# Fewer plain jobs in the dense stages, one square root behind the scatters, and row transfers that wait for the first gathers, in an attention and mixture-of-experts block

## What is computed

```
h = layernorm(x) * (1 + ca) + sa
x = x + ga * attention(h)          # 16 heads of 8 features, q = k = v = h, 2 x 16 x 1024 x 1024 scores
h = layernorm(x) * (1 + cb) + sb
shared = relu(h @ sW1 + sb1) @ sW2 + sb2
probs  = softmax(h @ router_W + router_b)      # 15 experts
cw     = the 3 largest of probs per token, 0 elsewhere
y      = sum over e of cw[e] * (relu(h @ eW1[e] + eb1[e]) @ eW2[e] + eb2[e])
x = x + gb * (shared + y)
```

## Time and profile before

| | |
|---|---|
| median of 3 runs | 377.3 us (375.74 to 377.87) |
| profiled execution | 377.16 us; span 375.6 us |
| PE, ACT, DVE, POOL busy | 86%, 76%, 44%, 22% of the span |
| attention ends | about 261 us |
| tail: 10 groups of tiles | about 267 to 310 us |
| tail: dense stages, gathers and sums | about 310 to 370 us |

### The profile page before, as it was taken

The page is one execution under the profiler, slowest core; times in us unless marked ns, Lnnn a source line. Parts: engine busy times, 40 slices in busy tenths (PEclk is TensorE's granted clock), DMA queues, the critical chain, the costliest instruction groups (busy, mean ns, idle before and its releaser), DMA issues.

```text
span 375.6 us, 6507 instructions
## 1 busy us (share of the span) xinstructions
PE 321.9 (86%) x2355; PEld 146.2 (39%) x2355; DVE 164.9 (44%) x508; ACT 286.2 (76%) x284; POOL 82.7 (22%) x105
## 2 busy tenths in 40 slices
PE   4879799998999999899998999997599299999822
PEld 2632222222333223233222223321478296767521
DVE  7993014235152372442622303500265079877942
ACT  3679889999999999999999999997165265443311
POOL 4891001601000000100000656700010000067730
PEclk9999989999999999999999999999699699999985
DMA  7788899151000799700000011124844897912211
GB/s 219 253 316 293 276 364 307 48 188 66 3 2 0 268 308 391 241 0 2 3 0 2 29 38 49 51 80 125 268 113 117 249 384 230 384 39 77 83 31 61
DMA packets 37908, 55.94 MB, mean 149 GB/s; under 512 B 3888, under 2 KB 20818, under 8 KB 37232
## 3 DMA queue, kind: packets, MB, share of 16 engines
q1 hardware_dynamic: 35900, 51.92, 41.3%
q0 software_dynamic: 1536, 3.16, 3.0%
q10 hardware_dynamic: 436, 0.39, 0.3%
HBM read 34.92 MB, written 22.51 MB: 153 GB/s over the span
## 4 chain that ended last, share of the span: by engine, by line
issue 28%; PE 18%; POOL 13%; SPq 11%; DMA 11%; DVE 9%; ACT 8%; ACTq 1%; POOLq 0%; DVEq 0%
PE acc L1653 8%; ACT prob L840 7%; POOL xs_d L767 6%; SPq L574 5%; PE slot L1558 4%; SPq L575 4%; POOL QQ L778 4%; DMA val<-cw_d 3%; DMA xs_d<-xtok,line 2%; POOL val L778 2%; DMA cw_d<-cwT 2%; DMA KK<-kw 1%; PE slot L1713 1%; POOL rstd L689 1%; DMA kw<-w1l 1%
## 5 line engine op out<-in xcount | busy, mean ns | idle before, releaser
L840 ACT ACTIVATE prob<-slot 128x1536 f32<-128x1536 f32 x171 | 233.5, 1489 | 8.8 <-PE slot L1558 8.3
L1653 PE MATMUL acc<-prob,val 128*18 128x512 f32 x1024 | 136.4, 605 | 2.7 <-DVE oT L1145 1.8
L1558 PE MATMUL slot<-QQ,KK 32*128 32x512 f32 (+1 forms) x768 | 92.9, 410 | 11.6 <-ACT prob L840 8.2
L1558 PEld LDWEIGHTS slot<-QQ,KK 32*128 32x128 f32 x768 | 43.9, 187 | 130.0 <-ACT prob L840 93.9
L689 POOL TENSOR_TENSOR rstd<-rstd,power 128x4 f32<-128x4 f32 (+1 forms) x6 | 7.4, 1241 | 198.9 <-DVE rstd L984 198.9
L869 ACT ACTIVATE ghi<-prob 128x512 fp32r<-128x512 f32 x26 | 16.4, 632 | 31.5 <-DVE prob L1383 31.5
L1653 PEld LDWEIGHTS acc<-prob,val 128*18 128x18 f32 x1024 | 17.4, 96 | 31.9 <-issue 28.9
L778 POOL DMA_INDIRECT QQ<-ys_d,line x16 | 16.0, 1001 | 58.8 <-DMA val<-cw_d 54.2
L767 POOL DMA_INDIRECT xs_d<-xtok,line x24 | 23.9, 996 | 7.3 <-issue 6.4
L1145 DVE COPY oT<-acc 128x512 f32<-128x512 f32 x8 | 5.5, 692 | 42.9 <-PE acc L1653 42.9
L896 ACT ACTIVATE prob<-slot,rows 128x128 f32<-128x128 f32 x38 | 10.9, 373 | 11.0 <-DMA ys_d<-prob 6.5
(11 more groups left out here) (282 smaller groups left out, 359.9 us busy)
## 6 DMA issues: line engine op xcount, KB each, us to landing
KK<-wcat SPq DMA_DIRECT2D x32, 128.0 KB, 2.0
KK<-kd SPq DMA_DIRECT2D x14, 256.0 KB, 5.6
QQ<-qd SPq DMA_DIRECT2D x14, 256.0 KB, 6.0
KK<-kw SPq DMA_DIRECT2D x14, 256.0 KB, 6.4
KK<-cw_d SPq DMA_DIRECT2D x3, 1024.0 KB, 7.5
xs_d<-ffT SPq DMA_DIRECT2D x1, 2580.0 KB, 14.6
rows<-xs_d SPq DMA_DIRECT2D x10, 258.0 KB, 4.1
ys_d<-prob SPq DMA_DIRECT2D x10, 256.0 KB, 5.3
```

What stands on the lines that cost most here:

```text
L840: nc.scalar.activation(ring[:, at:at + n * CH], slot[u % 2][:, 0:n * CH], ACT.Exp, scale=SCALE).then_inc(exp_done, 1)
L1558: return mm(dst, KK[n][r, s, c * M:(c + 1) * M], QQ[n][r, lo:hi], start=True, stop=True, tile_position=(32 * q, 0))
L1653: last = mm(acc[32 * q:32 * q + 2 * HV], val[:, b, n // 2, c, q, HV * odd:HV * odd + 2 * HV], prob[:, (G * cl + q) % RING], start=c == 0 a ...
```

## The change

Three places change. `PLAIN` shrinks from positions 0, 6 and 11 to position 0, so four of the 32 jobs become split jobs, and two loads of 64 KB into `w2p` at the program's start go. POOL serves two square roots of 512 tokens, not three, before the scatters, and two, not one, behind them. And in the tail POOL's gathers of stage 0 wait for chunks 0 to 3 alone, SP's chunk 4 waits for those gathers (`gath[0]`), and the gathers of stage 1 wait for chunks 4 to 7. DVE's sums of stage 0 move from jobs 24 and 25 to jobs 16 and 22, and the first two sums of stage 1 from job 30 to behind the last job.

```diff
-PLAIN = (0, 6, 11)
+PLAIN = (0,)
...
             routing(1)
+            sp.wait_ge(gath[0], 16 * QC * K)
             for k in range(CHUNKS, DENSE * CHUNKS):
                 row_chunk(k)
...
-            for _ in range(LAST):
+            for _ in range(SORTED):
                 root_guess(0, QC)
...
-            root_guess(0, QC)
+            for _ in range(SORTED, STAGES):
+                root_guess(0, QC)
             for k in range(YRING):
                 pool.wait_ge(y_wr[k], 16 * len(range(k, GROUPS, YRING)))
-            for k in range(DENSE * CHUNKS):
-                pool.wait_ge(rows_ld[k], 16 * len(row_buffers(k)))
             pool.wait_ge(pv_done, CLASSES)
             for s in range(SORTED):
+                for k in range(CHUNKS * s, CHUNKS * (s + 1)):
+                    pool.wait_ge(rows_ld[k], 16 * len(row_buffers(k)))
                 for k in range(K):
                     for i in range(QC * s, QC * (s + 1)):
                         p.indirect_dma_start(yacc[s][k][:, i % QC], None, ys_d, line_of(i, k)).then_inc(gath[s], 16)
...
-                if g == EXPERTS + 8:
+                if g == EXPERTS:
                     three_results(0)
-                if g == EXPERTS + 9:
+                if g == EXPERTS + 6:
                     stage_sum(0)
-                if g == EXPERTS + 14:
-                    three_results(1)
+            three_results(1)
             stage_sum(1)
```

## The result

| | before | changed |
|---|---|---|
| median | 376.86 us (375.74 to 377.87, 4 runs) | 355.11 us (354.47 to 359.01, 4 runs) |
| profiled execution | 377.16 us, span 375.6 us | 359.01 us, span 357.3 us |
| PE, ACT, DVE, POOL busy | 86%, 76%, 44%, 22% | 89%, 80%, 47%, 23% |

The ratio is 0.945 [0.939, 0.951]: 5.5% faster. Every ratio in this document compares executions in the chip's faster state alone, with a 95% interval in brackets. The prediction was 360.4 us with a range from 356.5.

A forecast was written before the change was run, and what follows sets the result against it. PE and ACT bound the attention; then two PE holes and late gathers. Groups end 14.4 us earlier, the series behind takes 63.4 us, not 65.8: span 358.8, plus 1.6 gives 360.4 us, range 356.5 to 368.5.

The forecast's parts named there:

- Scatters and SP: POOL's scatters run from 187.9 to 223.7 us, 21.0 us earlier, again taking 35.8 us; SP's weights follow from 226.0.
- Rival C: Scatters stretch beside DVE's work between 188 and 208 us; unit 146 and all behind it 6 us later, 366.4; chance 0.06.
- F: Whole kernel: the gain is cancelled by a wait not seen, 377 us; chance 0.03.
- The two holes and the clock: PE's waits before the first tile and at group 0's store go: 4.9 and 7.1 us; faster clock 1.2 and 2.0.
- Rival B: The second hole, at group 0's store, stays in part; in full 369.5 us; chance 0.12.
- The new wait: At unit 146 PE waits 1.1 us for stage 2's normalised rows; 1.0 us charged at the attention's end.
- Gathers of stage 0: In the tail, twelve gathers until DVE sees the last take 16.6 us, as stage 1's did before.
- Stores and chunks in: Behind job 2, stores and chunks 0 to 3 land after 6.6 us in place of 7.3, bounds 5 to 8.5.
- The series: Tail's gathers, chunks 4 to 7, gathers set the end at 349.3; dense stages' last gate comes 4 us earlier, at 344.9.
- Split for plain: Down products in the jobs: 1.22 us plain against 1.18 split on PE; DVE's added low parts covered; no effect.
- The end: From DVE's last instruction to the end of the span, 5.8 us as before.
- Rival D: Chunks and gathers 1 us less in each link, nothing lost at unit 146: 354 to 357 us; chance 0.06.

The follow-up runs named there:

- the repetition: The whole change run again unaltered on another chip, against the kernel before: 356.51 us, ratio 0.945 [0.942, 0.949].
- the root between: Changed kernel with stage 2's square root between the second and third round of scatters: 356.06 us, ratio to the kernel before 0.943 [0.940, 0.947].
- the roots alone: Kernel before with only stage 2's square root moved behind the scatters: 359.9 us, ratio 0.955 [0.951, 0.959].
- the turns alone: Kernel before with only SP's wait, POOL's split wait and the new places of DVE's sums: 373.61 us, ratio 0.994 [0.991, 0.997].
- plain alone: Kernel before with only the list of plain products cut to position 0: 374.02 us, ratio 0.994 [0.991, 0.997].
- the late sums: Changed kernel without SP's wait before chunk 4 and with stage 0's sums at jobs 24 and 25: 348.86 us, ratio to the kernel before 0.927.

## Why the prediction was right and where it was wrong

The order of the waits and what ends each was right; several sizes were not. The columns are the predicted profile, the changed kernel's first profile, the one of the repetition and the last one.

| us | predicted | first | repetition | last |
|---|---|---|---|---|
| end of the attention | 262.3 | 260.3 | 259.0 | 259.4 |
| from there to job 2 | 33.1 | 32.2 | 32.2 | 32.2 |
| to stores and chunks in | 6.6 | 8.7 | 7.4 | 8.7 |
| to the first gather | 0.8 | 0.8 | 0.8 | 0.8 |
| gathers of stage 0, as DVE sees them | 16.6 | 17.8 | 18.0 | 18.0 |
| chunks 4 to 7, and to the next gather | 13.3 | 13.2 | 12.9 | 13.2 |
| gathers of stage 1 | 16.6 | 16.6 | 16.8 | 16.4 |
| last sums of DVE | 3.7 | 3.5 | 3.5 | 3.5 |
| from there to the span's end | 5.8 | 4.2 | 4.6 | 4.4 |
| span | 358.8 | 357.3 | 355.2 | 356.5 |

- **Scatters and SP.** Right. From the copies at 186.93 to the end of the last issue at 221.60 it took 34.7 us, where 35.8 were taken over from before; the weights followed 2.3 us later, as before. Rivals C and F are out. The 1.1 us that it was shorter are one pause between rounds of 1.38 us where the kernel before had 2.39, and no scatter of 1.48 us, less 0.4 for slower first copies.
- **The two holes and the clock.** Right: 32.2 us against 33.1 to job 2, with the clock at 1.00. Rival B is out. Group 0's store went out at 270.07 (predicted 272.1), when SP had just issued the last weights. The 0.8 us charged for stage 3's routing were not paid: from the first tile to job 2 the only wait in PE's timeline is 0.39 us.
- **The new wait, "I charge 1.0 us at the end of the attention".** Wrong in size. The rows were ready at 223.31 + 1.11 = 224.42 and PE took them at 224.57. They were 2.2 us earlier than the predicted 226.6, by the 1.1 us above and by a front 1.1 us ahead of the earlier trace rows. With no wait (the kernel before, and the one with the root between) PE's scores behind the side work start 1.08 us after those ahead of it; in the three profiles of the changed kernel it is 1.23, 1.39 and 1.24 us. So the wait was 0.15 to 0.31 us.
- **Gathers of stage 0, "I take what stage 1 took", 16.6.** 1.2 to 1.4 us too little. The first took 1.48 us in place of 0.94, and seven of the others came every 1.40 us, not every 1.26 (last section).
- **Stores and chunks in, "with the chunks spread more evenly I take 6.6".** 0.8 to 2.1 us too little. The last store took 8.20 us to land, where the one of before took 6.8. Spreading the chunks bought nothing. The loads of chunks 4 to 7 took 12.5, 12.1 and 12.4 us from first issue to last landing, as the trace of before had it (12.3). The 10.8 us estimated beside it were not reached; by the sizes in the profile the five loads have 3840 KB, which is 3.93 MB, and the estimate would be 11.0.
- **The series.** Right: it sets the end, stage 1's wait for a gather ends at 349.62 (predicted 349.3), and the dense wait came as 5.26 + 3.57 us on DVE, 5.48 us on PE. But its rival, the dense stages, was closer than the 4 us predicted: DVE waited only 1.64, 0.69 and 1.58 us for the last gather.
- **Split for plain, "nothing".** The reading of the costs was loose. 610 and 394 ns are lengths of records that overlap. By the starts, a job with a plain product took PE 1.56 us and a split one 1.40 (kernel before, 318.3 to 322.7 us), so a split product is the cheaper one by 0.16 us. It didn't reach the end, which the gathers set.
- **The end, "to the end of the span ... 5.8", taken over from before.** 1.2 to 1.6 us too much. The three undisturbed profiles of the kernel before have 5.8, 5.5 and 5.9 us there; the roots alone 5.8, the turns alone 4.4 and 4.5, plain alone 3.1 and 3.7. So this stretch was shorter with either smaller part, by 1.3 and by 2.0 to 2.6 us. If that is no chance of these few profiles, it is half of what the turns gained alone, and all of what the plain list did. But it does not add up: the changed kernel has both and is only 1.3 us shorter here. What happens there is only the last two stores of the output: the issue of one took 1.42 us before and 0.62 us after. Why was not settled.
- **The base.** The three undisturbed profiles of the kernel before end the attention at 261.3, 262.8 and 260.0 us, those of the changed kernel (the one with the root between counted) at 260.3, 259.0, 258.9 and 259.4. In the sum this is 2 us, and I had reckoned everything from the 261.3.

The windows of 40 to 50 us show where executions part (columns as in the earlier trace rows). The kernel before, the turns alone, the late sums:
```profile
40.00:50.00 10.00, 7.93 (x57) 2.04 (x57) 0.92 (x6) 7.51 (x6) 0.00 (x0) 0.83 0.91 307
```
```profile
40.00:50.00 10.00, 9.04 (x77) 2.63 (x81) 1.31 (x8) 10.00 (x9) 0.00 (x0) 1.00 0.93 301
```
```profile
40.00:50.00 10.00, 8.10 (x53) 2.15 (x49) 0.00 (x0) 6.54 (x5) 0.00 (x0) 0.69 0.90 303
```
ScalarE is busy for 7.51, 10.00 and 6.54 of 10 us, at a clock of 0.83, 1.00 and 0.69, in kernels whose programs differ nowhere up to 185 us but for two early loads. The attention then ended at 261.3, 258.7 and 262.7. So single executions differ by 4 us at the end of the attention, whatever the change, and in this window alone ScalarE's busy time differs by 3.5 us. The fastest version has as late a front as the kernel before had at its latest (262.8). That the changed kernel was early four times and the one before late three times is most likely chance: with the front of the kernel before, the turns alone ended the attention at 258.7 and the roots alone at 259.8, and with the front of the changed one the late sums ended it at 262.7. For the shorter list of plain products it took 109.5 us from the end of the attention to the last sum, with 108.6, 108.4 and 111.3 before. Its 0.6% isn't in the jobs, and no run here ties it to the stores by a mechanism.

**The sum.** By the means of these profiles, the span fell from 376.5 to 356.2, by 20.3 us: 2.0 in the front (predicted a loss of 1.0), 17.0 between the cuts (109.4 to 92.4; predicted 17.9), and 1.3 behind the last sum (predicted 0).

**The step that failed.** Three terms of the sum were too large: the charge of 1.0 us at unit 146 (measured 0.15 to 0.31), the 5.8 us at the end (4.2 to 4.6), and the base of 261.3 us, taken from one profile (258.9 to 260.3 in the changed kernel). Between the cuts the good agreement is partly luck: the groups took 0.9 us less than predicted, and stores and gathers of stage 0 2.2 to 3.5 us more. The range was added up from three terms only: it had no room for the base, for the end, or for the routing's own bounds of 0 to 2 us. (Its upper end by those three terms is 365.2, not 365.5.)

These terms explain the profiles, not the whole miss. The mean span of the four profiles is 356.2 us, 2.6 below the predicted 358.8. The measured median of 355.11 us stands for a span of about 353.4, another 2.8 us lower, and lies in executions without a profile. In which stretch they were quicker stays open. Rival D named the right time, 354 to 357, but for links of the series that did not get shorter; only its "nothing is lost at unit 146" came nearly true.

## What to carry to other kernels

When an answer that only one stage needs is computed ahead of a long run of transfers, see what is queued behind its request: moving one square root of 1 us behind 24 scatters gave 4.5%. The turns and the plain list gave 0.6% each when alone, which a repetition of an unchanged kernel hardly tells from nothing, and 0.9% together on top of the square root. On the chip where the attention was stretched beside the scatters, the square root's gain was gone, by one execution of each kernel. Turn-taking between gathers and loads moves the wait: the run without it showed that the loads could be hidden (4 us), and the run with later sums that DVE's own order held 3 us more. In that fastest version DVE is busy for 4.8 to 5.0 of every 5 us from 325 to 345 us, so whether it would gain from a longer plain list again, with fewer low parts for DVE, is open: it wasn't run. Anchor a prediction on more than one profile, and give the start and the end of the span a spread of their own.

## What the runs showed of the hardware

Of stage 0's gathers, seven in a row took 1.09 to 1.10 us and came every 1.40 us, where most of the kernel before took 0.95 to 0.96 and came every 1.26. Timeline of DVE in the changed kernel beside the gathers at 306.44 and 307.84:
```profile
306.04 0.68 DVE L1393 SCALAR_TENSOR_TENSOR glo<-prob,ghi 128x512 fp32r<-128x512 f32 x1
306.77 0.75 DVE L1385 SCALAR_TENSOR_TENSOR prob<-slot,bcol,KK 128x512 f32<-128x512 f32 x1
307.44 0.68 DVE L1393 SCALAR_TENSOR_TENSOR glo<-prob,ghi 128x512 fp32r<-128x512 f32 x1
```
DVE's loop has a period of 1.40 us too, so POOL had fallen into step with it. In the kernel with the root between, the first six gathers beside the same loop still came every 1.26 us, and only from the seventh on every 1.40. Once DVE stopped at 314.5, they took 0.95 us again. In stage 1, where DVE's loop had a period of 1.26 us, ten of twelve took 0.94 to 0.96. So the price seems to depend on how the two loops stand to each other, not on DVE being busy alone.

The Trainium skill (SBUF — State Buffer, section "SBUF: two separate sides") says that the two engines take turns on a shared port pair. The trace fits this: a gather that falls into step with DVE's loop takes 0.14 us more, and the twelve of stage 0 took 1.2 to 1.4 us more than those of stage 1. Which of DVE's two instructions does it was not tried. Rival C's 6 us had no ground for a simpler reason: between 188 and 208 us DVE is busy for only 4.33 of 20 us, and the scatters beside that work, from 202 us on, took 0.95 to 0.96 us like the rest.
